# VectorE steps with one SBUF input in a post-norm attention and mixture-of-experts layer

## The reference

```python
q, k, v = (split_heads(x @ w.T) for w in (Wq, Wk, Wv))
scores = jnp.where(causal, (q @ k.T) * 8 ** -0.5, -jnp.inf)
x = layernorm(x + (softmax(scores) @ v) @ Wo.T)

s = sigmoid(x @ router_w.T)                     # 64 experts in 8 groups of 8
sfc = s + e_bias
group_scores = top_k(sfc.reshape(T, 8, 8), 2)[0].sum(-1)
gmask = the 4 best groups                       # masked = sfc there, 0 elsewhere
idx = top_k(masked, 8)[1]
w = 2.5 * s[idx] / (s[idx].sum(-1) + 1e-20)     # coef: w at idx, 0 elsewhere
h = silu(x @ Wg[e]) * (x @ Wu[e]) * coef[:, e]  # every expert e, dense
x = layernorm(x + sum_e h @ Wd[e] + shared(x))
```

## Time and profile before

| | us |
|---|---|
| median of 3 runs | 1030.04 (1029.47 to 1031.43) |
| profiled execution, its own time | 1028.34 |
| its span | 1026.3 |
| TensorE busy | 958.7 (93%) |
| VectorE busy | 810.6 (79%) |
| GpSimd busy | 623.0 (61%) |
| ScalarE busy | 463.4 (45%) |

### The profile page before, as it was taken

The page is one execution under the profiler, slowest core; times in us unless marked ns, Lnnn a source line. Parts: engine busy times, 40 slices in busy tenths (PEclk is TensorE's granted clock), DMA queues, the critical chain, the costliest instruction groups (busy, mean ns, idle before and its releaser), DMA issues.

```text
span 1026.3 us, 16151 instructions
## 1 busy us (share of the span) xinstructions
PE 958.7 (93%) x5014; PEld 576.6 (56%) x5014; DVE 810.6 (79%) x2438; ACT 463.4 (45%) x882; POOL 623.0 (61%) x666
## 2 busy tenths in 40 slices
PE   5799989999999899999999999999999999988996
PEld 2344456665666556665566555665566556655553
DVE  5666767799978997799977997789977986587554
ACT  2344445445444445444444444454444445433332
POOL 2432227674776557675676657765676567766774
PEclk8699999999999999999999999999999999999999
DMA  8441053323633254323623244322633322322331
GB/s 296 133 148 59 27 169 128 116 83 101 199 106 116 87 164 134 116 79 99 206 98 115 95 141 148 128 74 80 215 91 118 103 94 90 97 87 90 102 112 63
DMA packets 63077, 120.79 MB, mean 118 GB/s; under 512 B 7056, under 2 KB 34576, under 8 KB 62608
## 3 DMA queue, kind: packets, MB, share of 16 engines
q1 hardware_dynamic: 62992, 119.76, 36.3%
HBM read 97.32 MB, written 22.02 MB: 116 GB/s over the span
## 4 chain that ended last, share of the span: by engine, by line
PE 59%; DVE 30%; issue 5%; DMA 2%; POOL 2%; ACT 1%; SPq 0%; POOLq 0%; DVEq 0%
PE acc L614 7%; DVE max_out L912 6%; PE sm L531 6%; DVE hid L985 5%; PE st L549 5%; PE pg L490 5%; PE ob L561 4%; PE pu L490 4%; DVE hid L976 4%; PE pg L492 4%; PE pg L491 4%; PE pu L492 4%; PE pu L491 4%; PE acc L486 3%; PE acc L604 2%
## 5 line engine op out<-in xcount | busy, mean ns | idle before, releaser
L728 POOL TENSOR_TENSOR hid<-hid,coef_b 128x512 f32<-128x512 f32 x255 | 329.8, 1293 | 193.0 <-DVE hid L985 155.9
L677 ACT ACTIVATE hid<-pg 128x512 f32<-128x512 f32 x264 | 157.8, 598 | 363.8 <-PE pg L492 363.2
L912 DVE CUSTOM_DVE_ANT_0 max_out<-sm,causal_sb 128x128 bf16<-128x128 f32 (+3 forms) x512 | 236.7, 483 | 97.0 <-PE sm L531 95.5
L976 DVE SCALAR_TENSOR_TENSOR hid<-hid,pg 128x512 f32<-128x512 f32 x264 | 180.1, 682 | 84.3 <-ACT hid L677 84.3
L732 POOL TENSOR_TENSOR hid_lo<-hid,hid_hi 128x512 fp32r<-128x512 f32 x127 | 163.5, 1287 | 76.0 <-ACT hid_hi L684 74.7
L649 ACT ACTIVATE probs<-st 128x512 f32<-128x512 f32 (+1 forms) x384 | 187.6, 526 | 34.5 <-PE st L549 33.0
L985 DVE TENSOR_TENSOR hid<-hid,pu 128x512 f32<-128x512 f32 x256 | 174.4, 681 | 9.3 <-PE pu L492 5.3
L490 PE MATMUL pg<-x_hi,wg_hi 128*128 128x512 f32 x256 | 144.1, 563 | 16.9 <-DVE hid L976 16.8
L531 PE MATMUL sm<-k_stack,q_stack 72*128 72x128 bf16 (+3 forms) x512 | 138.4, 311 | 13.5 <-DMA k_stack<-k_rows_dram 9.1
L714 POOL TENSOR_SCALAR_AFFINE_SELECT probs<-probs 128x256 f32<-128x256 f32 x256 | 102.3, 424 | 75.3 <-ACT probs L649 74.9
L490 PE MATMUL pu<-x_hi,wu_hi 128*128 128x512 f32 x256 | 125.1, 488 | 10.5 <-DVE hid L985 10.4
(11 more groups left out here) (134 smaller groups left out, 1271.4 us busy)
## 6 DMA issues: line engine op xcount, KB each, us to landing
coef_b<-coef_dram SPq DMA_DIRECT2D x128, 512.0 KB, 3.9
q_rows_dram<-qk_parts SPq DMA_DIRECT2D x24, 384.0 KB, 3.3
k_rows_dram<-qk_parts SPq DMA_DIRECT2D x24, 384.0 KB, 3.6
q_stack<-q_rows_dram SPq DMA_DIRECT2D x64, 144.0 KB
k_stack<-k_rows_dram SPq DMA_DIRECT2D x64, 144.0 KB
xT_sb<-in_xT SPq DMA_DIRECT2D x8, 256.0 KB, 3.9
y<-in_x SPq DMA_DIRECT2D x8, 256.0 KB, 4.5
out<-out_sb SPq DMA_DIRECT2D x8, 256.0 KB, 2.7
```

The lines of the kernel that those rows point to most:

```text
L728: pool.tensor_tensor(hid[:, i % 3, :], hid[:, i % 3, :], coef_b[:, half % 2, j, :], ALU.mult)\
L912: last = dve.tensor_tensor_reduce(out=max_out[:, seg.nth(BANK_SM, task) % 2, col:col + wide], in0=sm_of(seg, task)[:, col:col + wide], in1 ...
L976: dve.scalar_tensor_tensor(hid[:, i % 3, :], hid[:, i % 3, :], 1.0, pg[:, :], ALU.add, ALU.mult).then_inc(a_done, 1)
```

## The change

Four edits to VectorE's steps, and what follows from them on the other engines:

1. **Routing.** The pairwise maxima and minima, which read every second element of a tile as two inputs of a `tensor_tensor`, become `tensor_reduce` over pairs with one input. The merges write what has to be compared next side by side (`both`), the two results of the tree go side by side into `top_two`, so that their sum is a reduction too. The copy into `g_keep` becomes a reduction over one element.
2. **Splits.** The cast of the rest of q and k (L884) becomes a `tensor_reduce` over one element with a bf16 output.
3. **First residual.** Its sum is written back to the PSUM bank `ob` instead of `y`. Statistics and `normalise` of the first norm read it there; the bank is released after the fourth normalised tile, and this one count stands in for `x1_done` at TensorE's `x1T` and at SyncE's load of the next token tile. The second norm keeps `y` in SBUF.
4. **Maxima.** Two bf16 parts instead of three: a `tensor_reduce` with negation, then a `scalar_tensor_tensor` of two SBUF inputs that writes the second part directly. The four steps of `mn` become two, at the places of the old first and last. The transpose has 32 columns instead of 48, the DMA of rows 2 instead of 3 for each head.

```diff
@@ -34,6 +34,7 @@
 SPLIT_BY_DVE = 3
 CHUNKS = 9
 PARTS = 3
+MAX_PARTS = 2
...
-GROUP = {'mn': (-0.22, -0.15, 0.02, 0.14), 'mT': 0.42, 'pv': 0.05, 'ot': 0.67, 'on': 0.99}
-PACKED_GROUP = {'mn': (-0.22, -0.2, -0.182, 0.19), 'mT': 0.42, 'pv': 0.1, 'ot': 0.57, 'on': 1.19}
+GROUP = {'mn': (-0.22, 0.14), 'mT': 0.42, 'pv': 0.05, 'ot': 0.67, 'on': 0.99}
+PACKED_GROUP = {'mn': (-0.22, 0.19), 'mT': 0.42, 'pv': 0.1, 'ot': 0.57, 'on': 1.19}
...
-        max_rest = sb("max_rest", [P, HG * NT])
-        max_parts = sb("max_parts", [P, PARTS, HG * NT], BF16)
-        max_rows = sb("max_rows", [PARTS * HG * NT, P], BF16)
+        max_parts = sb("max_parts", [P, MAX_PARTS, HG * NT], BF16)
+        max_rows = sb("max_rows", [MAX_PARTS * HG * NT, P], BF16)
...
-        merge_tmp = sb("merge_tmp", [P, NT * NG * 2])
+        both = sb("both", [P, NT * NG * 2, 2])
+        top_two = sb("top_two", [P, NT, NG, 2])
...
-                        after(sp, seg, x1_done, ("x1",), seg.last(("x1",), task))
+                        before = seg.last(("x1",), task)
+                        if before:
+                            after(sp, seg, ob_free, BANK_O, ("oproj", before[1], 0))
...
-                        dst = q_stack[QK_ROWS:QK_ROWS + PARTS, HG * i % RING:HG * i % RING + HG, :]
+                        dst = q_stack[QK_ROWS:QK_ROWS + MAX_PARTS, HG * i % RING:HG * i % RING + HG, :]
...
-                        pe.transpose(sm[0:PARTS * HG * NT, 0:P // 2].bitcast(BF16),
+                        pe.transpose(sm[0:MAX_PARTS * HG * NT, 0:P // 2].bitcast(BF16),
...
-                            after(pe, seg, x1_done, ("x1",), ("x1", n, NT - 1))
+                            after(pe, seg, ob_free, BANK_O, ("oproj", n, 0))
...
+            y_bank = ob[:, :].rearrange("p (t d) -> p t d", t=NT)
+
+            def add_residual(seg, task, out, x_in):
                 after(dve, seg, ob_full, BANK_O, task)
-                dve.tensor_tensor(y[:, :, :].rearrange("p t d -> p (t d)"), ob[:, :],
-                                  x_in.rearrange("p t d -> p (t d)"), ALU.add).then_inc(ob_free, 1)
-
-            def norm_step(seg, i, task):
+                return dve.tensor_tensor(out.rearrange("p t d -> p (t d)"), ob[:, :],
+                                         x_in.rearrange("p t d -> p (t d)"), ALU.add)
+
+            def norm_step(seg, i, task, src):
 
                 if i == 0:
-                    after(dve, seg, ob_free, BANK_O, task)
+                    if task[0] == "oproj":
+                        ready("y")
+                    else:
+                        after(dve, seg, ob_free, BANK_O, task)
                     for t in range(NT):
-                        last = dve.bn_stats(stats[:, t, :], y[:, t, :])
+                        last = dve.bn_stats(stats[:, t, :], src[:, t, :])
                     done(last, "ln")
                 elif i == 1:
                     ready("ln")
@@ -778,29 +786,29 @@
                     ready("ln")
                     dve.tensor_scalar(var_eps[:, :], mv[:, :, 1], EPS, None, ALU.add).then_inc(var_done, 1)
 
-            def normalise(seg, task, t, dst, s):
+            def normalise(seg, task, t, dst, src):
                 if t == 0:
                     after(dve, seg, rstd_done, LN, task)
-                dve.tensor_scalar(dst[:, t, :], y[:, t, :], mv[:, t, 0:1], rstd[:, t:t + 1],
-                                  ALU.subtract, ALU.mult).then_inc(s, 1)
...
-            def pairs_of(ap, many):
-
-                both = ap[:, 0:many].rearrange("p (g e) -> p g e", e=2)
-                return both[:, :, 0], both[:, :, 1]
-
-            def merge(many, hi, lo, hi_out, lo_out):
+            def of_pairs(out, ap, many, op):
+
+                return dve.tensor_reduce(out, ap[:, 0:many].rearrange("p (g e) -> p g e", e=2), AX_X, op)
+
+            def merge(many, hi, lo, hi_out):
 
                 m = many // 2
-                dve.tensor_tensor(merge_tmp[:, 0:m], *pairs_of(lo, many), ALU.max)
-                dve.tensor_tensor(hi_out[:, 0:m], *pairs_of(hi, many), ALU.max)
-                return dve.tensor_tensor(lo_out[:, 0:m], *pairs_of(hi, many), ALU.min)
+                of_pairs(both[:, 0:m, 0], lo, many, ALU.max)
+                of_pairs(both[:, 0:m, 1], hi, many, ALU.min)
+                return of_pairs(hi_out, hi, many, ALU.max)
 
             def merge_rest(many, lo_out):
-                m = many // 2
-                return dve.tensor_tensor(lo_out[:, 0:m], lo_out[:, 0:m], merge_tmp[:, 0:m], ALU.max)
+                return dve.tensor_reduce(lo_out, both[:, 0:many // 2, :], AX_X, ALU.max)
+
+            firsts, seconds = (top_two[:, :, :, e].rearrange("p t g -> p (t g)") for e in range(2))
...
-                    dve.tensor_tensor(pair_hi[:, :], *pairs_of(sfc, NT * E), ALU.max)
-                    last = dve.tensor_tensor(pair_lo[:, :], *pairs_of(sfc, NT * E), ALU.min)
+                    of_pairs(pair_hi[:, :], sfc, NT * E, ALU.max)
+                    last = of_pairs(pair_lo[:, :], sfc, NT * E, ALU.min)
                 elif i == 3:
-                    last = merge(NT * E // 2, pair_hi, pair_lo, quad_a, quad_b)
+                    last = merge(NT * E // 2, pair_hi, pair_lo, quad_a[:, :])
                 elif i == 4:
-                    last = merge_rest(NT * E // 2, quad_b)
+                    last = merge_rest(NT * E // 2, quad_b[:, :])
                 elif i == 5:
-                    last = merge(NT * E // 4, quad_a, quad_b, pair_hi, pair_lo)
+                    last = merge(NT * E // 4, quad_a, quad_b, firsts)
                 elif i == 6:
-                    last = merge_rest(NT * E // 4, pair_lo)
+                    last = merge_rest(NT * E // 4, seconds)
                 elif i == 7:
-                    last = dve.tensor_tensor(gs[:, :, 0:NG], pair_hi[:, 0:NT * NG].rearrange("p (t g) -> p t g", t=NT),
-                                             pair_lo[:, 0:NT * NG].rearrange("p (t g) -> p t g", t=NT), ALU.add)
+                    last = dve.tensor_reduce(gs[:, :, 0:NG], top_two[:, :, :, :], AX_X, ALU.add)
                 elif i == 8:
                     last = each_tile(lambda t: dve.max(g_top[:, t, :], gs[:, t, 0:NG]))
                 elif i == 9:
-                    last = dve.tensor_copy(g_keep[:, :, 0:TOPG], g_top[:, :, 0:TOPG])
+                    last = dve.tensor_reduce(g_keep[:, :, 0:TOPG], g_top[:, :, 0:TOPG].unsqueeze(3), AX_X, ALU.max)
...
-                            done(dve.tensor_copy(parts[:, 1, :], rest[:, :]), kind)
+                            done(dve.tensor_reduce(parts[:, 1, :], rest[:, :].unsqueeze(2), AX_X, ALU.max), kind)
...
-                        g, step = divmod(i, 4)
+                        g, step = divmod(i, MAX_PARTS)
                         rm = row_max[:, g % 2, :, :].rearrange("p h t -> p (h t)")
                         if step == 0:
 
                             after(dve, seg, sm_free, BANK_SM, ("mx", n, 3 * (HG * g + HG) - 1))
-                            done(dve.tensor_scalar(max_parts[:, 0, :], rm, -1.0, None, ALU.mult), "mn")
-                        elif step == 1:
-                            ready("mn")
-                            done(dve.scalar_tensor_tensor(max_rest[:, :], rm, -1.0, max_parts[:, 0, :],
-                                                          ALU.mult, ALU.subtract), "mn")
-                        elif step == 2:
-                            ready("mn")
-                            done(dve.tensor_copy(max_parts[:, 1, :], max_rest[:, :]), "mn")
+                            done(dve.tensor_reduce(max_parts[:, 0, :], rm.unsqueeze(2), AX_X, ALU.max, negate=True), "mn")
                         else:
                             ready("mn")
-                            dve.tensor_tensor(max_parts[:, 2, :], max_rest[:, :], max_parts[:, 1, :],
-                                              ALU.subtract).then_inc(maxparts_done, 1)
+                            dve.scalar_tensor_tensor(max_parts[:, 1, :], rm, -1.0, max_parts[:, 0, :],
+                                                     ALU.mult, ALU.subtract).then_inc(maxparts_done, 1)
...
-                        add_residual(seg, task, y[:, :, :])
+                        done(add_residual(seg, task, y_bank, y[:, :, :]), "y")
                     if kind == "ln":
-                        norm_step(seg, i % 3, ("oproj" if i < 3 else "finT", n, 0))
+                        norm_step(seg, i % 3, ("oproj" if i < 3 else "finT", n, 0), y_bank if i < 3 else y)
                     if kind == "x1":
-                        normalise(seg, ("oproj", n, 0), i, x1[:, par], x1_done)
+                        last = normalise(seg, ("oproj", n, 0), i, x1[:, par], y_bank)
+                        if i == NT - 1:
+                            last.then_inc(ob_free, 1)
...
-                        add_residual(seg, task, x1[:, par])
+                        add_residual(seg, task, y[:, :, :], x1[:, par]).then_inc(ob_free, 1)
```

11 lines of the change are left out of this document (6 added, 5 removed).

## The result

| | before | after |
|---|---|---|
| median of the runs compared, us | 1029.76 (1026.61 to 1031.43, 4 runs) | 999.75 (999.03 to 1002.3, 4 runs) |
| ratio, 95% interval | | 0.9725 [0.9706, 0.9744] |
| profiled execution, its own time | 1028.34 | 1002.3 |
| its span | 1026.3 | 1000.2 |

The change takes 2.7% off. The profiled execution of after is the slowest of its four, so traces differ by 26.1 us and medians by 30.0. The sum was made for the traces and said 27.2.

The account below looks back on a forecast made before the run. VectorE was taken as the bound in 30 us of layer norm and routing. Routing and residual 18.2, maxima 7.7, casts 2.4, less 1.1 at the start: 27.2 us off, 1001.1 profiled, median 1003; eight in ten 989 to 1021.

Parts of the forecast that it names:

- Rival D: Reductions wait for GpSimd too, so waits stay and the change does not do what it says: 1030 us, chance 0.03.
- The price of a reduction: A pair reduction on VectorE costs by its inputs, 1.02 ns a column; 0.70 us added to the routing per batch.
- Rival C: A `tensor_reduce` pays for each output; at 3.5 ns per output 15 us slower, 1045 us, chance 0.06.
- PSUM: First norm's four normalising steps reading PSUM wait for nobody: 692 to 400 ns each, a gain of 1.2 us per batch.
- the 64 columns (65 ns) that I had set aside: First norm's normalising steps: 64 columns more from PSUM if half are free from SBUF, making 464 ns; 400 was taken.
- Tail: Routing 1.4 and first residual 1.2 us per batch, 2.6 x 7 tails beside the experts = 18.2 us.
- the seven steps that still wait: Seven routing instructions keep forms that wait for GpSimd, 2.7 us at worst, 0 at best; 1.0 us given back.
- rival B: TensorE's own chain takes over behind tail and groups; half of residual and maxima lost: 1011 us, inside the forecast's 0.67.
- Maxima: Two of four head groups count on the chain, 0.6 and 0.5 us: 1.1 per batch, 7.7 us over seven.
- The 0.4 that I took off for the moved step: Group at 513 us: the moved two-input instruction may meet GpSimd itself, 0.4 us, leaving 0.6 net of 1.0.
- Casts and start: Casts gain 0.4 us in each of six batches, 2.4; dearer forms in the first batch, GpSimd idle, cost 1.1.
- rival A: The waits move: remaining waiting forms on VectorE catch nearly all that is freed, 1013 to 1024 us, chance 0.18.

Follow-up runs that it names:

- the forms by themselves: A kernel writing zeros, not the layer: eight VectorE instructions of each form, GpSimd idle, then beside its 512-column products; two SBUF inputs: 286 to 1080 ns.

## Why the prediction was right

**The cause.** VectorE's instructions with two SBUF inputs wait for GpSimd's, and so do its scalar operations and casts from SBUF to SBUF. Reductions don't, and neither do the two forms with an input from PSUM. The waits were inferred from one pair of rows and three comparisons (the earlier trace rows with the earlier trace rows), and both halves are shown by the forms by themselves. The Trainium skill (SBUF — State Buffer, Who interferes with whom) had the word "never" for `tensor_reduce`; the runs agree, 410 and 405 ns without and with GpSimd at work. Rival D falls with it.

**The price of a reduction.** By its inputs, (414 - 284)/128 = 1.02 ns a column: forecast 414 for the pairs and 674 for the casts, measured 403 to 410 and 671 to 680. Rival C, a price per output, falls: 128 outputs from 256 inputs cost no more than L852's 4 outputs.

**PSUM.** 400 ns forecast, 402 measured, and the four steps give 2.77 - 1.61 = 1.16 us (1.2 forecast). Alone the residual is worth 1.31 us in pairs 24 to 27. That the 400 was met has luck in it. I called the 399 ns of the earlier trace rows undisturbed. They are the mean of 356, 472, 436 and 333 ns, beside four masks of GpSimd's from 109.51 to 111.03 us. The step's own time is about 330 ns, as the shortest of the 32 before shows (min, median and max):

```profile
L784 DVE TENSOR_SCALAR x<-y,mv,rstd x32: 330/396/1327, 110.0 to 909.0; 128x128 f32<-128x128 f32 x32
```

The move to PSUM does cost this step some 70 ns, about the 64 columns (65 ns) that I had set aside, and a base that was too high by as much covered for it. The 120 cycles of the Trainium skill (VectorE: DVE Perf Modes, The TRN2 errata) against 58 don't show: the statistics of 128 columns have a median of 279 ns from PSUM and 276 from SBUF in after, the form with one input from PSUM takes 278 ns against 286 for two from SBUF, and this step needs 398 in SBUF, too, where it accumulates.

**Tail.** Forecast 2.6 per batch for residual and routing, after 1.0 was given back to the seven steps that still wait. Measured 1.93 + 0.90 = 2.83, of it 1.31 by the residual alone and 0.63 + 0.90 by the routing alone (1.4 forecast); the maxima alone move these pairs by 0.02 net. The seven didn't lengthen: `th` has a median of 768 ns (759), `sfc` 505 (506), `chosen` 588 (588), and all seven together take 3.03 us in the mean of the first six tails beside the experts (3.02). The give-back came from chance arrivals, but this is one static order, and in both kernels these steps meet the same products; the share of them that waits had to be read from their own rows and was no new cost. So the 1.0 had the wrong reason, and that the sum of the tail came out near is luck. About as much was lost elsewhere. VectorE's busy time in the two stretches falls by 2.43 + 1.73 = 4.16 us, of which 1.3 don't reach the time: TensorE is busy 29.95 of 30.62 us there now (30.75 of 33.45 before), and its own work is what is late next, which is rival B in a small size.

**Maxima: the term that was mis-sized.** Beside units 8/9 I forecast 0.6 and got 0.69, by the right cover (the tanh). `a` started 1.59 us after the start of the tanh and starts 0.63 after it now, so the gain there is 0.96, as I had counted (1.0). The 0.4 that I took off for the moved step did not arise: it waits 0.25 us, and with the step back ahead of `a` the pair stays at 5.36. The rest is lost behind `a`, for a reason that no run shows. Beside units 17/18 I forecast 0.5, the step L926 shorter by 0.59, and got 0.01. I had allowed for the tanh at the one group and forgot it at the other: in the chain of after, the 0.61 us of L680 stand where L926 stood, and `a` starts no earlier. So the maxima are worth 0.7 and not 1.1 in these two places, until the wait of 1.04 us behind goes, too (the kernel with all of the maxima by reductions, and the one with the second step moved, both -0.8).

**Casts and start.** 0.4 a batch forecast, and 3.92 - 0.69 - 0.01 - 2.83 = 0.4 is left for them and the stage that they stand in. Here rival A came true in part. In the batch of the earlier trace rows the second cast falls from 1.50 to 0.68 us, and the second norm's first step behind it comes 1.4 us earlier in the batch. It now comes at the start of GpSimd's next product and not at its end, and takes 1.37 us instead of 0.71. The casts are what does it, since the four steps have a mean of 654 ns with the casts alone and of 553 to 556 with each of the other three parts alone. The prediction named these four steps as ones that could catch a wait, and put no such cost into its sum. At the start 1.1 us of dearer forms were forecast. The experts start 0.62 later, but the traces don't show that this is them: with the residual alone, which adds none, they start 1.69 later than before, and with the routing alone, to which 0.70 of it belong, 0.95 earlier.

**The sum.** 27.2 us against 26.1 in the spans, with the tail 0.2 a batch better and the maxima 0.4 worse; that these nearly cancel is luck, too. The forecast set the median 1.7 us above the profiled execution, and for after it lies 2.6 below. That makes 4.3 us; less the 1.1 by which the sum was too good, they are the 3.2 between 1003 and 999.75. VectorE's busy time fell by 47.3 and not 42 us. The maxima's steps fell by 32 x (464 + 470 + 166 + 347 - 167 - 457) ns = 26 us and not 20, since the old last step took 347 ns on average and not 170.

## What to carry to other kernels

Look in the order of time for the same instruction at two durations, and for what the other engines did at the long one, before you shorten the work in it. Where GpSimd works beside it, a VectorE step that costs more cycles with one SBUF input can be the cheaper one, and two waiting steps behind each other deserve it most. Then ask at each place what the next instruction waits for besides: a wait that fits under another engine's work is worth nothing, and one 2 us later in the same group may be worth 0.8. And look at the step behind each one that you shorten: if it keeps a form that waits, it may come in front of the same product.

## What the runs showed of the hardware

- GpSimd is held up too, though less. Its product of 512 columns takes 1255 ns with VectorE at rest, 1305 to 1377 beside VectorE's steps with two SBUF inputs and 1437 to 1449 beside its casts. All 60 in the kernel of the forms by themselves, min, median and max in ns:

```profile
L74 POOL TENSOR_TENSOR g_out<-g_a,g_b x60: 1255/1263/1449, 22.8 to 96.7; 128x512 f32<-128x512 f32 x60
```

- A scalar operation of 128 columns takes 339 ns in SBUF while GpSimd rests. From PSUM it takes 400 and 397 ns, without and with GpSimd at work, and with an accumulated output in SBUF 398.
- A reduction over one element as a cast of 512 columns takes 673 ns against the cast's 417, so by itself it pays only where the cast would wait by more than 256 ns.
